# Two message stages of a graph network: SyncE reads a table's fields for three steps with one register load, without bounds checks

## The reference, cut to what matters

```
h = jnp.maximum(_layernorm(x, axis=-1), 0.0)
w = act(edge_feature @ W_fc1) @ W_fc2           # per edge
xs, xv = s[dst], v[dst]                         # gather the other end's features
out0a = w0 * xs
out0b = w3 * (jnp.einsum('emi,ei->em', xv, sh1) * INV_SQRT3)
out1a = (w1 * xs)[:, :, None] * sh1[:, None, :]
out1b = w2[:, :, None] * xv
out1c = w4[:, :, None] * (jnp.cross(xv, sh1[:, None, :]) * INV_SQRT2)   # layer 1 alone
agg = jax.ops.segment_sum(tp, src, num_segments=N)
x = x + (skip(h) and gate(agg @ W_out))
```

## Time and profile before

| | us |
|---|---|
| median of 3 runs | 10501.72 |
| the profiled execution | 10502.67 |
| its span, first to last instruction | 10500.9 |
| messages of layer 0 | 2312 to 6940 |
| messages of layer 1 | 7489 to 10214 |

### The profile page before, as it was taken

How to read it: one execution, slowest core, us unless ns; L and a number is a source line. 1 busy time by engine, 2 the same in 40 slices (tenths; PEclk the granted TensorE clock), 3 DMA queues, 4 the chain that set the end, 5 groups by cost and what they waited for, 6 DMA issues and landing times. The chain is left out here.

```text
span 10500.9 us, 206215 instructions
## 1 busy us (share of the span) xinstructions
PE 7559.7 (72%) x42550; PEld 6214.4 (59%) x42550; DVE 7302.1 (70%) x20592; ACT 5171.9 (49%) x16292; POOL 7155.5 (68%) x7101
## 2 busy tenths in 40 slices
PE   5555565557777777777777777775888888888868
PEld 3333333336666666666666666664677777777767
DVE  7555555556666666666666666656799998889963
ACT  3444444434444444444444444430266666666643
POOL 4777777777777777777777777730377777777740
PEclk8555555558887778778777778886799999999999
DMA  2222222234444444444444444651455555555575
GB/s 89 89 90 90 89 89 90 90 96 134 136 134 135 135 135 135 136 134 135 134 137 135 135 135 136 131 109 55 115 153 153 153 154 152 151 153 152 152 114 176
DMA packets 841838, 1325.45 MB, mean 126 GB/s; under 512 B 228020, under 2 KB 642228, under 8 KB 841140
## 3 DMA queue, kind: packets, MB, share of 16 engines
q0 software_dynamic: 339456, 670.10, 23.7%
q1 hardware_dynamic: 441188, 590.81, 20.4%
q10 hardware_dynamic: 60624, 59.64, 2.2%
HBM read 868.00 MB, written 918.54 MB: 170 GB/s over the span
## 5 line engine op out<-in xcount | busy, mean ns | idle before, releaser
L1156 POOL DMA_INDIRECT feat_m<-feat_tab,rows_m x3744 | 3796.3, 1014 | 1905.7 <-issue 1061.4
L1265 ACT ACTIVATE hot_m<-hot_m,rows_m 128x128 f32<-128x128 f32 x11232 | 3483.6, 389 | 3112.0 <-DVE hot_m L1383 3092.0
L1247 PE MATMUL bank<-prod_m,hot_m 128*128 128x96 f32 (+1 forms) x14976 | 2503.4, 335 | 1298.3 <-DVE prod_m L1404 1282.7
L1247 PEld LDWEIGHTS bank<-prod_m,hot_m 128*128 128x128 f32 x14976 | 2364.0, 236 | 1696.9 <-issue 1626.8
L1247 PE MATMUL pair<-prod_m,hot_m 128*128 128x160 f32 x14976 | 2265.0, 304 | 463.3 <-DVE prod_m L1404 383.0
L1247 PEld LDWEIGHTS pair<-prod_m,hot_m 128*128 128x128 f32 x14976 | 2065.7, 190 | 662.8 <-issue 662.7
L1404 DVE TENSOR_TENSOR prod_m<-rows_m,feat_m 128x192 f32<-128x192 f32 x5616 | 1557.2, 317 | 873.2 <-DMA feat_m<-feat_tab,rows_m 872.6
L602 POOL DMA_INDIRECT sorted_rows<-rows_e,place_e x1664 | 1671.3, 1004 | 533.0 <-issue 525.2
L1173 POOL DMA_INDIRECT sorted_rows<-later_m,place_m x1664 | 1680.8, 1010 | 507.0 <-issue 472.3
L1397 DVE TENSOR_TENSOR prod_m<-rows_m,feat_m 128x128 f32<-128x128 f32 x3744 | 913.0, 284 | 201.5 <-DMA feat_m<-feat_tab,rows_m 190.2
L1383 DVE SCALAR_TENSOR_TENSOR hot_m<-iota_n,base_node,rows_m 128x256 f32<-128x256 f32 x1872 | 899.4, 480 | 35.6 <-issue 12.5
(11 more groups left out here) (209 smaller groups left out, 7541.6 us busy)
## 6 DMA issues: line engine op xcount, KB each, us to landing
agg_tab<-acc_m SPq DMA_DIRECT2D x936, 320.0 KB
rows_m<-sorted_rows SPq DMA_DIRECT2D x936, 229.0 KB
agg_tab<-acc_m SPq DMA_DIRECT2D x936, 224.5 KB
rows_m<-sorted_rows SPq DMA_DIRECT2D x936, 197.0 KB
feat_m<-feat_tab,rows_m POOLq DMA_INDIRECT x3744
turned_m<-in_turned ACTq DMA_DIRECT2D x211, 256.0 KB
agg_s<-agg_tab SPq DMA_DIRECT2D x98, 320.0 KB, 2.8
sorted_rows<-rows_e,place_e POOLq DMA_INDIRECT x1664, 2.4
```

What stands on the lines that cost most here:

```text
L1156: pool.indirect_dma_start(out=feat[s % RING][:, k, :], out_offset=None, in_=g.feat_tab[l.n], in_offset=bass.IndirectOffsetOnAxis(ap=rows[s ...
L1247: mm = pe.matmul(dst, hot[s % HOTS][:, k, q, :], rhs, start=(k == 0 and col == 0), stop=(k == ST_TILES - 1), skip_group_check=True)
L1265: ins = act.activation(hot[s % HOTS][:, k, 1 + q, :], hot[s % HOTS][:, k, 0, :], ACT.Copy, scale=rows[s % RING][:, k, l.sh_at + q:l.sh_at ...
```

## The change

`g.table` gets rows of three fields, without the unused fourth, and one row more, so that its rows can be read three at a time. SP reads nine registers (three steps) every third step, ahead of that step's waits, and keeps them in `fields` until they are used. The checks of the values against their limits are left out. What is loaded and stored stays the same.

```
+READ = 3
+assert TURN % READ == 0 and (NST + STORE_LAG + 1) % READ == 0
-        g.table = sb("table", [1, NST + STORE_LAG, 4], I32)
+        g.table = sb("table", [1, NST + STORE_LAG + 1, 3], I32)
...
+            fields = []
+
+            def read(u):
+
+                _, regs = nc.values_load_multi_w_load_instructions(
+                    g.table[0:1, bass.ds(u, READ), :].rearrange("p o c -> p (o c)"), engines=[mybir.EngineType.SP],
+                    min_val=0, max_val=E_PAD - ST,
+                    skip_runtime_bounds_check_because="the table's rows are cut off at E_PAD - ST and the rest is smaller")
+                fields[:] = [regs[3 * k:3 * k + 3] for k in range(READ)]
+
             def step_(step, it, s):
                 u = it * TURN + s
+                if s % READ == 0:
+                    read(u)
                 loads = step is None or step < NST
                 if loads and (step is None or step >= RING):
                     sp.wait_ge(hot_scaled, u - RING + 1)
                     sp.wait_ge(prod_ready, u - RING + 1)
                     settle(sp, g.passed)
-                _, (row, blk, last) = nc.values_load_multi_w_load_instructions(
-                    g.table[0:1, bass.ds(u, 1), 0:3].rearrange("p o c -> p (o c)"), engines=[mybir.EngineType.SP],
-                    min_val=0, max_val=E_PAD - ST)
+                row, blk, last = fields[s % READ]
```

## The result

The changed kernel takes 10477.6 us (median of 20 runs, 10460.7 to 10495.9) where the kernel before takes 10501.7 on the same chips: a ratio of 0.998, 95% interval 0.9973 to 0.9986. It is faster, by 24 us. I had forecast 10360, a gain of 142, and a range from 10325 to 10440; the time lies above that range.

The account below looks back on a forecast made before the run. The prediction took SP to pace layer 1's main part, POOL to saturate layer 0. Savings of 128 (main part), 13 (last part) and 1 (starts), 142 us off 10502.67, gave 10360 us, range 10325 to 10440.

Parts of the forecast that it names:

- Layer 0 gives nothing: Layer 0 loop: POOL is saturated and SP waits for sums, so a faster SP saves 0 us.
- SP paces layer 1, and leaves the path: Layer 1, main part: SP sets the pace; its step falls from 2.69 to 1.51 us, below POOL's 2.678.
- The nine-field read, 1.0 us: SP's table read, once in three steps: taken as 1.0 us, 0.38 us a step with address and gaps.
- upper bound of 2.02: SP's nine-field read if each field pays: 3 x 0.672 = 2.02 us, still leaving SP's step below POOL's.
- POOL, 2.678 us a step if its gathers keep their mean of 1034 ns: Layer 1, main part: POOL's limit once SP is faster, two gathers a step at 1.339 us each.
- my sum: Layer 1, main part: 871 steps falling from 2.847 to 2.70 us, 128 us saved.
- 2.70: Layer 1, main part: forecast step in us, slightly above POOL's limit and the DVE and PE loop's 2.68.
- The rival "slower": Both layers: bunched loads and stores lengthen indirect DMAs; 27 ns more cancels the gain, +40 ns gives 10571 us; 3%.
- Coupling worse: Layer 1, main part: POOL and the DVE and PE loop couple worse, 2.76 us a step, 10412 us; 22%.
- The last part, 13 us: End of layer 1: a round trip shorter by 1.26 us, shared by six steps, saves 0.21 us a step, 13 us.
- The starts: Starts of two stages: only the first load counts, 0 to 1 us saved for each, 1 us together.

Follow-up runs that it names:

- two_reads_c: The kernel before with each three-field read split into one of one field and one of two, checks kept: 10640.0 us, 1.0121.
- no_checks: The kernel before with only its bounds checks left out, still one read of three fields a step: 10447.7 us, 0.9953.
- read3_checked: The changed kernel with its bounds checks kept, nine behind each nine-field read: 10704.9 us, 1.0196.
- psum_after: The changed kernel with layer 1's products taking their first factor from PSUM, not the loaded rows (output not the reference's): 10374.0 us, 0.9885.

## Why the prediction was wrong, step by step

- *Layer 0 gives nothing*: right. 3520 and 3525 DMAs in the stretch; SP only waits longer, 2977.5 instead of 1811.8 us.
- *SP paces layer 1, and leaves the path*: right. two_reads_c shows the first, SP's waits of 954.0 us (forecast some 900) the second.
- *The nine-field read, 1.0 us*: wrong size. It is 1.87 in three of four cases, near the upper bound of 2.02. The bound was said to do no harm, as a mean of SP's step; but the read stands in one piece, and no_checks without it is 30 us faster than the change. Of these 30, 8 ns a step (7 us) are shorter gathers, 2 x (1075 - 1071), the rest POOL waiting less. That the bunches of loads do this is argued from the timeline; read3_checked shows the same at a larger size.
- *"POOL, 2.678 us a step if its gathers keep their mean of 1034 ns"*: this is the step that failed. They did not keep it; 1075 ns makes 2.760 us, and the 0.059 us idle left on top 2.818. Put into my sum, 871 x (2.847 - 2.818) = 25 us in place of 128. Of the 0.118 us a step between 2.70 and 2.818, 0.082 are the longer gathers and 0.036 is waiting beyond what I allowed for. The mean of an instruction that contends with another engine is not a property of it: it moved from 1034 to 1075 when POOL came around at other times of DVE's step, and to 954 when DVE's second SBUF input went away. psum_after brings the step back to 2.70.
- *The rival "slower"* priced longer gathers at a wrong place: 27 ns on all indirect DMAs of both layers, put down to traffic. They rose by 41 ns in layer 1 alone (layer 0: 997 and 1015 now, 997 and 1010 before), the traffic is the same (154 GB/s against 153), and the cause is DVE. Its right half, that a gain of SP can be paid back in gathers, had 3% and deserved more.
- *Coupling worse* (2.76 us a step) named the two servers but not that one lengthens the other's work; the measured 2.818 lies beyond it too.
- *The last part, 13 us*: not seen, 3.54 us a step over the last 63 steps, 3.56 before. I had said that the wait behind SP ends last there. It does not: SP waits 120.6 us instead of 58.8, and the pace stays. The DMA engines are busy for 83% of the time there at 108 GB/s, for 56% at 153 GB/s in the main part, so by these figures a byte takes 2.1 times the busy time; whether the transfers set the pace was not tried. *The starts*: six loads in 4.88 us instead of 10.36; the first gather comes at 7489.39 instead of 7492.66, but with it the layer's whole schedule, and the 1 us put on them can't be told apart.

## What to carry to other kernels

Freeing the engine that paces a stage shifts when the others begin, so look, before adding up, whether the next limit's duration depends on what runs beside it: sort its instructions by what the other engine was doing, and take the mean that the new phase will give. A serial engine's step is not a mean either: work gathered into one piece must be held against the depth of the ring that it feeds. Of two edits in one change, time each alone; here leaving the checks out beats the whole, and the fastest version that computes the layer with its loaded weights is no_checks, 10447.7 us. And compare stretches of equal steps, not of equal times, where a stage ends with a slower part or begins later.

## What the runs showed of the hardware

- SP's register loads of the table in layer 1 took, by their medians, 0.277 us for one field and 0.477 for two (two_reads_c, 7520 to 9960), 0.672 for three (the kernel before, 7500 to 9980) and 1.867 for nine (the changed kernel, 7500 to 9980). 0.07 us + 0.2 a field fits these four. But in each layer of the changed kernel the first nine-field read and every fourth one from it on, 79 of 314, were shorter: 0.741 to 0.766 us in layer 1, where the other 235 took 1.862 to 1.889, and 0.742 to 0.977 in layer 0. Why these are shorter was not shown.
- In layer 1 of the changed kernel (7500 to 9980) a gather issued by POOL took 0.945 us on average if it began beside the sum, whose `pair` lies in PSUM, and 0.946 beside nothing, never over 0.96. In psum_after it took 0.945 beside products with one input in PSUM. In the changed kernel it took up to 2.17 if it began among products with both inputs in SBUF, and up to 2.50 beside the one-hot just ahead of them. The 243 over 1.3 us ended 0.81 to 0.83 us behind the last product of the run, not of the product beside which they began. DVE's products hardly lengthened: those of 192 elements took 353 ns on average there and 350 in psum_after.
